# Four graph layers with norms: sums taken by the adding pass, squares on ScalarE, the turned adjacency loaded, and new due times for the plan

## What is computed

```python
x = _layernorm(x + L0(x, adj))   # 12-head attention, masked by adj > 0
x = _layernorm(x + L1(x, adj))   # two graph convolutions; exp(u)*adj, inner norm, relu
x = _layernorm(x + L2(x, adj))   # two directed convolutions; softmax*adj, inner norm, relu
x = _layernorm(x + L3(x, adj))   # 12-head attention, adj added, and an output projection
# _layernorm: (x - mean) / sqrt(var + 1e-5) over the 384 features
```

## Time and profile before

| what | us |
|---|---|
| median of 3 runs | 2745.75 (2744.03 to 2746.03) |
| the profiled execution | 2747.06 |
| its span, first to last instruction | 2745.3 |
| TensorE busy | 2590.6 (94%) |
| VectorE busy | 2315.3 (84%) |
| GpSimd busy | 2123.3 (77%) |
| ScalarE busy | 1758.2 (64%) |

### The profile page before, as it was taken

How to read it: one execution, slowest core, us unless ns; L and a number is a source line. 1 busy time by engine, 2 the same in 40 slices (tenths; PEclk the granted TensorE clock), 3 DMA queues, 4 the chain that set the end, 5 groups by cost and what they waited for, 6 DMA issues and landing times.

```text
span 2745.3 us, 90305 instructions
## 1 busy us (share of the span) xinstructions
PE 2590.6 (94%) x33792; PEld 1932.8 (70%) x33792; DVE 2315.3 (84%) x8232; ACT 1758.2 (64%) x4628; POOL 2123.3 (77%) x3211
## 2 busy tenths in 40 slices
PE   5899889999999999999999999999999999989996
PEld 4677667767677777777777777777776777667764
DVE  6789887879888888888888888888888888888877
ACT  6646666556666666666666666666666565666546
POOL 6577868777788788888788888888887777777675
PEclk9899999999999999999999999999999999999997
DMA  7733454344444544544545454454554453354315
GB/s 175 157 71 79 81 94 81 74 77 78 89 84 76 95 81 84 94 88 78 89 87 91 83 96 82 80 93 88 88 81 75 82 93 70 77 90 95 60 37 107
DMA packets 800731, 238.95 MB, mean 87 GB/s; under 512 B 767664, under 2 KB 799536, under 8 KB 800304
## 3 DMA queue, kind: packets, MB, share of 16 engines
q1 hardware_dynamic: 791840, 218.23, 44.8%
q10 hardware_dynamic: 8464, 14.94, 1.8%
HBM read 31.72 MB, written 12.58 MB: 16 GB/s over the span
## 4 chain that ended last, share of the span: by engine, by line
PE 54%; DVE 19%; POOL 11%; issue 5%; DMA 5%; ACT 4%; SPq 2%; DVEq 0%; POOLq 0%; ACTq 0%
PE bank L848 7%; PE bank L849 7%; PE bank L850 7%; PE bank L839 6%; PE bank L840 6%; PE bank L841 6%; DMA region<-region 3%; DVE region L1024 3%; PE bank L935 2%; PE bank L878 2%; PE bank L928 2%; PE bank L936 2%; POOL region L644 2%; POOL ab L671 2%; PE bank L864 1%
## 5 line engine op out<-in xcount | busy, mean ns | idle before, releaser
L839 PE MATMUL bank<-region,w_hi 128*128 128x128 f16 x3960 | 687.7, 220 | 7.4 <-DMA region<-region 2.6
L840 PE MATMUL bank<-region,w_hi 128*128 128x128 f16 x3960 | 686.6, 220 | 0.0
L841 PE MATMUL bank<-region,w_lo 128*128 128x128 f16 x3960 | 686.6, 220 | 0.0
L848 PE MATMUL bank<-w_hi,region 128*128 128x384 f16 x1815 | 596.5, 329 | 30.2 <-DMA region<-region 20.7
L849 PE MATMUL bank<-w_lo,region 128*128 128x384 f16 x1815 | 595.6, 328 | 0.0
L850 PE MATMUL bank<-w_hi,region 128*128 128x384 f16 x1815 | 595.6, 328 | 0.0
L655 POOL TENSOR_TENSOR region<-region 128x512 f16<-128x512 f32 x330 | 383.9, 1164 | 185.9 <-ACT region L776 184.1
L770 ACT ACTIVATE region<-region,small 128x128 f32<-128x128 f32 x1320 | 419.5, 392 | 79.3 <-DVE small L1030 61.1
L839 PEld LDWEIGHTS bank<-region,w_hi 128*128 128x128 f16 x3960 | 389.0, 98 | 32.5 <-issue 7.7
L840 PEld LDWEIGHTS bank<-region,w_hi 128*128 128x128 f16 x3960 | 388.8, 98 | 12.3 <-issue 5.8
L841 PEld LDWEIGHTS bank<-region,w_lo 128*128 128x128 f16 x3960 | 388.8, 98 | 0.0
(11 more groups left out here) (217 smaller groups left out, 7742.0 us busy)
## 6 DMA issues: line engine op xcount, KB each, us to landing
region<-region SPq DMA_TRANSPOSE x715, 3.1
last_unit<-w_dram ACTq DMA_DIRECT2D x19, 576.0 KB, 6.1
x<-x_dram SPq DMA_DIRECT2D x55, 192.0 KB, 2.6
out_dram<-region SPq DMA_DIRECT2D x55, 192.0 KB, 2.1
adj<-adj_dram SPq DMA_DIRECT2D x55, 64.0 KB, 2.3
rows<-rows_dram ACTq DMA_DIRECT2D x5, 576.0 KB, 4.4
last_unit<-last_unit SPq DMA_TRANSPOSE x117, 3.1
last_unit<-x_dram SPq DMA_DIRECT2D x9, 192.0 KB, 2.5
```

The lines of the kernel that those rows point to most:

```text
L839: pe.matmul(dst, lhsT=w_hi[:, w, k, cols], rhs=t_hi[u][:, k, :], start=(k == 0), stop=False)
L840: pe.matmul(dst, lhsT=w_hi[:, w, k, cols], rhs=t_lo[u][:, k, :], start=False, stop=False)
L841: last = pe.matmul(dst, lhsT=w_lo[:, w, k, cols], rhs=t_hi[u][:, k, :], start=False, stop=(k == DT - 1))
L848: pe.matmul(dst, lhsT=t_hi[u][:, k, :], rhs=w_hi[:, w, k, :], start=(k == 0), stop=False)
```

## The change

Three things. First, `turn_adj` leaves TensorE and ScalarE: the host hands over the transposed adjacency as another input, and SyncE loads it (`load_adj`) into the same tile after the same wait; GpSimd's part keeps its two instructions under the name `sides`. Second, in the four residual norms and in inner norms 2 and 3 bn_stats and bn_aggr go. The adding pass on VectorE (`residual`, and line 1090 in `inner`) also puts out its sum (`accum_out`). ScalarE then makes minus the mean (a Copy of one column), and a Square of the 384 values with that column as bias, whose sum goes to a column (`spread`, `inner_spread`); the squares themselves go to a scratch tile. GpSimd divides that sum by 384 in the instruction that adds eps. The centring pass of inner norms 2 and 3 becomes a part of its own, `centre`, that waits for the Square. Inner norms 0 and 1 are as before. Third, every due time is new: `PERIOD` is 20.108, the table has other values, and the shifts, for graphs 0 to 15 and 50 to 63, are eight each, one for each stage of a graph. `PARTS` and `SHIFTED` are cut here to a few rows.

```diff
--- before.py
+++ after.py
-PERIOD = 41.9385
...
+PERIOD = 20.1080
...
+SHIFTED = {
+    0: (-214.647, -123.076, -82.970, -144.420, -205.803, -198.625, -397.860, -243.257),
+    1: (2.746, -8.453, 4.931, -1.139, 6.274, 8.107, -14.342, 6.813),
...
+    63: (-89.478, -153.904, -82.402, -13.188, -17.199, -14.780, -182.063, -142.972),
+}
...
-    (PE, "turn_adj", 0): (-32.725, 0.120, 0.380, ((VECTOR, "scores", 2),), ()),
-    (SCALAR, "turn_adj", 0): (166.828, 0.156, 0.426, ((PE, "turn_adj", 0),), ()),
-    (POOL, "turn_adj", 0): (360.920, 0.875, 1.060, ((SCALAR, "turn_adj", 0), (PE, "attend", 2)), ()),
-    (VECTOR, "residual", 1): (291.165, 1.280, 1.430, ((VECTOR, "gain", 1),), ()),
-    (PE, "project", 18): (-1235.989, 1.466, 1.660, ((SYNC, "turn", 6),), ()),
-    (PE, "scores", 0): (109.959, 0.360, 0.610, ((VECTOR, "project", 2), (POOL, "low", 0), (POOL, "low", 1)), ()),
...
+    (SYNC, "load_adj", 0): (-211.757, 0.450, 2.500, ((VECTOR, "scores", 2),), ()),
+    (POOL, "sides", 0): (-160.488, 0.875, 1.060, ((SYNC, "load_adj", 0), (PE, "attend", 2)), ()),
+    (VECTOR, "residual", 1): (261.088, 0.580, 0.750, ((VECTOR, "gain", 1),), ()),
+    (SCALAR, "spread", 1): (-149.650, 0.830, 0.950, ((VECTOR, "residual", 1),), ()),
+    (SCALAR, "inner_spread", 3): (-141.438, 0.800, 0.920, ((VECTOR, "inner", 3),), ()),
+    (VECTOR, "centre", 3): (348.903, 0.463, 0.560, ((SCALAR, "inner_spread", 3),), ()),
+    (PE, "project", 18): (-73.086, 1.466, 1.660, ((SYNC, "turn", 6),), ()),
+    (PE, "scores", 0): (-215.748, 0.360, 0.610, ((VECTOR, "project", 2), (POOL, "low", 0), (POOL, "low", 1)), ()),
...
+def stage_of(part):
+
+    _, name, k = part
+    if name in ("project", "add_bias", "bias", "low"):
+        return 0 if k < 3 else k // 3 + 1 if k < 18 else 7
+    if name in ("turn", "residual", "norm", "spread"):
+        return {"turn": (0, 2, 3, 4, 5, 6, 7)}.get(name, (1, 3, 5, 7))[k]
+    if name in ("scores", "attend"):
+        return 1 if k < DT else 7
+    if name in ("divide", "bias_x"):
+        return 7 if k else 1
+    if name in ("u_di", "delta_di", "turn_delta", "sums", "delta", "delta_low"):
+        return 4 + k
+    if name in ("u_gcn", "delta_gcn", "mix", "inner", "inner_spread", "centre", "gain"):
+        return 2 + k
+    return {"load": 0, "masks": 0, "load_adj": 2, "sides": 2, "turn_adj": 2, "minus_adj": 6, "store": 7}[name]
 
 
...
-            wanted[part, i] = i * PERIOD + SHIFTED.get(i, 0.0) + at
+            wanted[part, i] = i * PERIOD + (SHIFTED[i][stage_of(part)] if i in SHIFTED else 0.0) + at
...
+            def load_adj(i, k):
+                sp.wait_ge(*topped.at(i, HG - 1, DT - 1))
+                sp.dma_start(adj_t[i % UNITS], adj_t_d[i]).then_inc(adj_t_landed.of(i), 16)
...
             def inner(i, k):
                 u = i % UNITS
-                pool.wait_ge(*numbers.at(i, "inner mv", k))
                 if k < 2:
+                    pool.wait_ge(*numbers.at(i, "inner mv", k))
                     pool.tensor_tensor(col(u, ROOT), mv[u][:, 1:2], constant(HALF), ALU.pow).then_inc(gpsimd_done.of(i), 1)
                 else:
+                    pool.wait_ge(*scalar_done.at(i, "inner spread", k))
                     pool.wait_ge(*gpsimd_done.at(i, "constant", k - 2))
-                    pool.tensor_tensor(col(u, VAR), mv[u][:, 1:2], col(u, EPS), ALU.add).then_inc(gpsimd_done.of(i), 1)
+                    pool.tensor_scalar(col(u, VAR), col(u, SQUARES), 1.0 / D, col(u, EPS), ALU.mult, ALU.add)\
+                        .then_inc(gpsimd_done.of(i), 1)
                     pool.wait_ge(*gpsimd_done.at(i, "variance", k))
                     pool.tensor_tensor(col(u, ROOT), col(u, VAR), constant(MINUS_HALF), ALU.pow).then_inc(gpsimd_done.of(i), 1)
 
             def residual(i, layer):
                 u = i % UNITS
-
-                pool.wait_ge(*numbers.at(i, "residual mv", layer))
-                pool.tensor_tensor(col(u, VAR), mv[u][:, 1:2], constant(LN_EPS), ALU.add).then_inc(gpsimd_done.of(i), 1)
+                pool.wait_ge(*scalar_done.at(i, "spread", layer))
+                pool.tensor_scalar(col(u, VAR), col(u, SQUARES), 1.0 / D, 1e-5, ALU.mult, ALU.add).then_inc(gpsimd_done.of(i), 1)
                 pool.wait_ge(*gpsimd_done.at(i, "shifted variance", layer))
                 pool.tensor_tensor(col(u, ROOT), col(u, VAR), constant(MINUS_HALF), ALU.pow).then_inc(gpsimd_done.of(i), 1)
                 pool.wait_ge(*gpsimd_done.at(i, "root", layer))
-                pool.tensor_scalar(col(u, SHIFT), mv[u][:, 0:1], col(u, ROOT), -1.0, ALU.mult, ALU.mult)\
-                    .then_inc(gpsimd_done.of(i), 1)
+                pool.tensor_tensor(col(u, SHIFT), col(u, MINUS_MEAN), col(u, ROOT), ALU.mult).then_inc(gpsimd_done.of(i), 1)
 
...
-            def turn_adj(i, k):
-                act.wait_ge(*multiplied.at(i, "adj"))
-                act.activation(adj_t[i % UNITS], bank("turn_adj", k, i)[:, 0:N], ACT.Copy).then_inc(scalar_done.of(i), 1)
-
             def norm(i, layer):
                 u = i % UNITS
                 act.wait_ge(*gpsimd_done.at(i, "residual root", layer))
                 act.activation(out[u] if layer == 3 else x[u], z[u], ACT.Identity, bias=col(u, SHIFT), scale=col(u, ROOT))\
                    .then_inc(scalar_done.of(i), 1)
 
+            def spread(i, layer):
+                u = i % UNITS
+                act.wait_ge(*mixed_out.at(i, "added", layer))
+                act.activation(col(u, MINUS_MEAN), col(u, SUM), ACT.Copy, scale=-1.0 / D).then_inc(scalar_done.of(i), 1)
+                act.wait_ge(*scalar_done.at(i, "minus mean", layer))
+                act.activation(score_at[u], z[u], ACT.Square, bias=col(u, MINUS_MEAN), accum_out=col(u, SQUARES))\
+                   .then_inc(scalar_done.of(i), 1)
+
+            def inner_spread(i, k):
+                u = i % UNITS
+                act.wait_ge(*numbers.at(i, "summed", k))
+                act.activation(col(u, MINUS_MEAN), col(u, SUM), ACT.Copy, scale=-1.0 / D).then_inc(scalar_done.of(i), 1)
+                act.wait_ge(*scalar_done.at(i, "inner minus mean", k))
+                act.activation(score_at[u], inner_of(i, k), ACT.Square, bias=col(u, MINUS_MEAN), accum_out=col(u, SQUARES))\
+                   .then_inc(scalar_done.of(i), 1)
+
...
-            def turn_adj(i, k):
-
-                pe.wait_ge(*topped.at(i, HG - 1, DT - 1))
-                bank_is_read(i, "turn_adj", k)
-                pe.transpose(bank("turn_adj", k, i)[:, 0:N], adj[i % UNITS], ident).then_inc(multiplied.of(i), 1)
-
...
                 dve.wait_ge(*multiplied.at(i, "mixed", k))
                 if k >= 2:
                     dve.wait_ge(*numbers.at(i, "diagonal", k - 2))
-                    dve.scalar_tensor_tensor(made[:, 0:D], proj[u][1], col(u, DIAGONAL), made[:, 0:D], ALU.mult, ALU.add)\
-                       .then_inc(numbers.of(i), 1)
-                    dve.wait_ge(*numbers.at(i, "summed", k))
+                    dve.scalar_tensor_tensor(made[:, 0:D], proj[u][1], col(u, DIAGONAL), made[:, 0:D], ALU.mult, ALU.add,
+                                             accum_out=col(u, SUM)).then_inc(numbers.of(i), 1)
+                    return
                 dve.bn_stats(st6[u], made[:, 0:D]).then_inc(numbers.of(i), 1)
-                if k < 2:
-                    dve.tensor_scalar(col(u, DENOM3), made[:, D:D + 1], 1e-10, 1e-3, ALU.add, ALU.mult)\
-                       .then_inc(numbers.of(i), 1)
+                dve.tensor_scalar(col(u, DENOM3), made[:, D:D + 1], 1e-10, 1e-3, ALU.add, ALU.mult).then_inc(numbers.of(i), 1)
                 dve.wait_ge(*numbers.at(i, "inner st", k))
                 dve.bn_aggr(mv[u], st6[u]).then_inc(numbers.of(i), 1)
                 if (k, i) == first(VECTOR, "inner", k):
                     dve.wait_ge(rows_loaded[piece_of(GAIN_ROW[k])], 16)
                 dve.wait_ge(*numbers.at(i, "inner mv", k))
                 dve.scalar_tensor_tensor(inner_of(i, k), made[:, 0:D], mv[u][:, 0:1], rows[:, GAIN_ROW[k], :], ALU.subtract, ALU.mult)\
+                   .then_inc(numbers.of(i), 1)
+
+            def centre(i, k):
+                u = i % UNITS
+                if (k, i) == first(VECTOR, "centre", k):
+                    dve.wait_ge(rows_loaded[piece_of(GAIN_ROW[k])], 16)
+                dve.wait_ge(*scalar_done.at(i, "inner spread", k))
+                dve.scalar_tensor_tensor(inner_of(i, k), inner_of(i, k), col(u, MINUS_MEAN), rows[:, GAIN_ROW[k], :], ALU.add, ALU.mult)\
                    .then_inc(numbers.of(i), 1)
 
...
                 if layer == 0:
                     dve.wait_ge(*low_made.at(i, "biased", 0))
                     dve.wait_ge(*mixed_out.at(i, "o", 0))
-                    dve.tensor_tensor(z[u], o[u], x[u], ALU.add).then_inc(mixed_out.of(i), 1)
+                    dve.scalar_tensor_tensor(z[u], o[u], 1.0, x[u], ALU.mult, ALU.add, accum_out=col(u, SUM)).then_inc(mixed_out.of(i), 1)
                 elif layer < 3:
```

(44 more changed lines are left out.)

371 lines of the change are left out of this document (173 added, 198 removed), and 27 rows, old and new, of the table SHIFTED.

## The result

The median of the changed kernel is 2730.66 us (2730.06 to 2737.0, 5 runs), against 2745.75 (2743.16 to 2748.16, 5 runs): a ratio of 0.9948, 95% interval 0.9934 to 0.9961. So it is faster, by 15 us or half a percent, where 50 was forecast. The profiled execution took 2730.39 us around a span of 2728.5, 16.8 less than the span before. Two single executions further down were far slower at a lower granted clock (narrow_gpsimd 2940.6 us at 0.84, load_halves 3695.9 at 0.65), and the medians given for these two kernels leave them out.

A forecast was written before the change was run, and what follows sets the result against it. TensorE, 94% busy, was taken as the bound. Transposes 7, order 40 (flanks 33, middle 5, ends 2) and clock 4, less chain 1, made 50 off 2747: 2697, median 2695; own range 2672 to 2715, reaching 2655 to 2742.

The forecast's parts named there:

- rival (a): The new order gives nothing, only the transposes and their waits are gained: 2725 us, chance 0.20.
- (e): Rival: the plan comes out with the same hold-ups in other places, so no change: 2745 us, chance 0.06.
- Transposes leave TensorE, 7, and the clock, 4: On TensorE: 64 adjacency transposes gone gain 7 us; a better granted clock gives back 4 us.
- Flanks, 33: TensorE's idle time from 300 to 900 and 2100 to 2500 us, 66.0 us, is halved: 33 us gained.
- The middle, 5 gained: TensorE from 900 to 2100 us, idle 13.0 us: the new order gains 5 us.
- The ends, 2 gained: TensorE's idle time in the first 300 us and after 2500 us: the new order gains 2 us.
- VectorE to 2060: VectorE's busy time falls from 2315 to about 2060 us, 75%, as the statistics leave it.
- ScalarE to 2102, 0.94 us a norm: ScalarE's column copy, Square and accumulator read add 0.94 us a norm, 361 us in all; busy time becomes 2102 us, 77%.
- GpSimd, 13 more: GpSimd: two inner norms' instructions grow from 0.20 to 0.305 us, 13 us more; the residual's exchange costs nothing; 78%, no bound.
- Rival (d): Square needs another table set: two loads a norm on ScalarE, 985 us, some 3100 us in all; chance 0.02.
- Rival (c): Square pairs on ScalarE delay line 760's copies out of PSUM and TensorE waits: slower, 2778 us, chance 0.10.
- The load, cost 0: The turned adjacency's 64 load issues on SyncE's queue are hidden: cost 0, or up to 28 us without cover.

The follow-up runs named there:

- narrow_gpsimd: The changed kernel in its own order, with the two GpSimd bias passes beside the masks cut to 8 of 384 columns: 2700.83 us, ratio 0.9826 to before.
- load_halves: masks_later with the turned adjacency loaded in two halves of 64 columns, 64 issues more on SyncE's queue: 2712.40 us, ratio 0.9864 to before.
- masks_later: The changed kernel with the two mask instructions moved later in VectorE's order in 31 graphs, behind projection 2's low part: 2704.64 us, ratio 0.9852 to before.
- no_shifts: The changed kernel planned without any stage shifts, period and table of due times kept: 2736.02 us, ratio 0.9962 to before.
- squares_twice: masks_later with every Square and its sum run a second time on ScalarE: 2813.19 us, ratio 1.0229 to before.
- stats_back: The changed kernel in its own order with bn_stats and bn_aggr back on VectorE and no squares on ScalarE: 2818.74 us, ratio 1.0264 to before.

## Why the prediction was off

The direction and the range (2655 to 2742) held; the size did not, 50 us against 15, and 2730.7 is outside the forecast's own range of 2672 to 2715. What is near it in the prediction is rival (a) with 2725, but its mechanism, an order that gives nothing in the flanks, is not what happened. Two ends of the ranges don't follow from their terms either: 2742 is said to reach to (e), which is 2745, and with all of the flanks gained the forecast would be 2662 and not 2672. Against the span's 16.8 the sum of 50 is 33.2 too high: 20.8 in the middle, 11.2 in the ends and 2.7 in busy time, less 0.5 and 1.0 in the flanks and the chain. By its own steps:

- **Transposes leave TensorE, 7, and the clock, 4**: busy time fell by 8.3 where the two made 11. It fits, but it isn't shown: no run parts one from the other, and with the same instructions TensorE is busy 8.8 us less still in masks_later and 9.2 less in no_shifts, so an order alone moves this number by as much as the term. The granted clock over the span is 0.985 before and 0.986 after.
- **Flanks, 33**: 33.5. Right, with luck: half of 66 was a choice between a quarter and all, no row priced it, and the planner's simulation gives 15.7. The runs show where it comes from: the due times together with the relief, not the stage shifts (no_shifts).
- **The middle, 5 gained: this is the step that failed.** It lost 15.8. I took the middle as full and safe, since 13.0 us of idle time over 1200 left little to win, and asked only how much an order can give. I never asked whether the new order would be as tolerant as the old one. It repeats itself graph by graph, so the two masks were held up in nearly every one of 29 graphs. masks_later and narrow_gpsimd both bring the middle back, to 10.3 and 11.4 us, by removing one contention. With the middle mended the kernel stands at 2704.6, 10 us from the forecast of 2695. That this is so near is partly luck: its busy time is 17.1 us under that of before, where I had 11, and its ends still lose.
- **The ends, 2 gained**: they lost 9.2, 5.0 of it from 100 to 300 us and 5.8 after 2500, less 1.6 gained before 100. The planner's simulation has the ends 10.3 us longer, so the loss comes with the order, and I could have read it there. no_shifts shows that the shifts matter there. Which part of the new due times does it stays open. In the drain TensorE waits most for DMA transposes. From 2500 us of after:

```profile
PE bank L964 <- DMA region<-region: 7.5, 5, 1.9
PE bank L921 <- DMA region<-region: 5.3, 2, 4.0
```

- **VectorE to 2060**: 2077.7, and 2055.6 in masks_later. The 22 us between are 29.8 of held-up masks less the 10.6 of line 1123, and small change. The rows of before had the sign of it: two of the adding passes differ by 0.24 us in the mean (lines 1124 and 1127), the slower one being the one with both operands on SBUF, and the longest of line 997 above is 1204 ns against a median of 352. I read the first as a property of the form, but its shortest is 537 ns, so most of the difference is hold-ups.
- **ScalarE to 2102, 0.94 us a norm**: 2046.5, so with the 17.4 of line 785 gone (2046.5 - 1740.8)/384 = 0.80. The groups by line and shape of after:

```profile
L856 ACT ACTIVATE region<-z,small 128x384 f32<-128x384 f32 x220 | 135.4, 615 | 7.1
L864 ACT ACTIVATE region<-bank,small 128x384 f32<-128x384 f32 x110 | 64.0, 582 | 3.6
L854 ACT ACTIVATE small<-small 128x1 f32<-128x1 f32 x220 | 43.2, 196 | 57.2 <-DVE z L1200 29.4 <-DVE z L1205 14.1 <-DVE z L1197 13.3
L856 ACT ACTIVATION_READ_ACCUMULATOR region<-z,small 128x1 f32 x220 | 41.0, 187 | 0.0
...
L817 ACT ACT_TABLE_LOAD x1 | 1.3, 1283 | 2.4 <-issue 2.4
```

  The three durations are as estimated (0.20, 0.61, 0.198), to 0.01, or 0.03 for a Square out of PSUM; what was too small is their overlap, 0.2 us where I took 0.07.
- **GpSimd, 13 more**: 2117.1, which is 6.2 less. The terms missed: the shift's tensor_scalar of 0.28 us became a tensor_tensor of 0.195 (256 x 0.085 = 22 less), while the tensor_scalar that adds eps takes 0.200, as the tensor_tensor before it did, so the exchange in the residual was a gain and not nothing. In the inner norms it is 0.271, so 9 more and not 13. It bounds nothing here.
- **Rival (d), Square in another table set**: one load, as before. The reading of the Trainium skill's rule on table sets (ScalarE: Activation LUTs, "Table sets: the hidden batching unit") by which Square would be outside the set doesn't hold: 384 Squares run between Exp, Copy, Relu and Identity without a second load.
- **Rival (c), through ScalarE's queue**: not at this load, but squares_twice shows the price of a second Square: 0.28 us at the end for each (108/384), and not the 0.94 that I took for one in front of a copy. What the first costs no run shows by itself, since stats_back changes VectorE as well; in the middle it is within the 10.3 us of masks_later.
- **The load, cost 0**: holds, to within the 8 us of load_halves.

## What to carry to other kernels

Before an order is called full, look for instructions whose longest duration is far above their median, and see what runs beside them; an order that repeats turns a rare meeting into one for each tile, and a planner with fixed costs doesn't see it. What such a planner does see is worth reading before a forecast: here its own ends differed by 20 us, and by stretches it had the loss in the ends. Two halves of a change that were made for each other can't be priced apart by putting each in alone. Doubling a new cost once tells how near its engine is to the edge, which a busy share of 76% doesn't.

## What was not expected of the hardware

A VectorE pass of 0.35 us with two tensors from SBUF takes 0.99 us when a GpSimd pass of 1.00 us has begun just before it, and a `tensor_scalar` of 0.22 us took 1.01. With the GpSimd passes 8 columns wide the first is back at 0.356. The Trainium skill has the rule (SBUF — State Buffer, "Who interferes with whom"): a VectorE instruction with two SBUF inputs, or in a mode that uses two ports, contends with GpSimd for a port pair that they share, and in such a mode the one that issues first has the pair for its whole instruction while the other is fully blocked. The trace agrees for the form with two inputs and for the `tensor_scalar`: in the middle of after the held ones end 0.07 to 0.16 us after the GpSimd pass. In which mode the `tensor_scalar` ran no row shows. VectorE's passes out of PSUM don't show it: line 1070 of after, 384 columns with one operand in PSUM, took 0.55 us at 1508.95 with a GpSimd pass begun at 1508.43 beside it, and the longest of its 128 runs is 0.559.
